# The stores of turned tiles leave the queue of the loads

## The chip, the cores and the metric

The kernel runs on one core of one Trainium2 chip. The metric is device time in microseconds (us) for one execution of the whole program, as a median of several runs. The profile is of one further execution, and its times count from the start of its span. A transfer between the chip's memory (HBM) and the core's own memory is issued by an engine, and carried by 16 DMA engines that serve all queues of the core.

## The reference

A stack of four graph layers works on features x of 5120 nodes by 64 and one matrix adj of 5120 by 5120, all float32. Each layer normalises its input and adds its result to x:

```
h = relu(layernorm(x));  x = x + L0(h, adj)     # e = h + par*(diag*h) @ W
                                                # layernorm(adj @ (adj.T @ e)) * gamma + beta + h
h = relu(layernorm(x));  x = x + adj @ h        # L1
h = relu(layernorm(x));  x = x + L2(h, adj)     # Chebyshev: three products adj @ T, with weights
h = relu(layernorm(x));  x = x + L3(h, adj)     # relu(D^-1/2 (adj + I) D^-1/2 (h @ W + b))
```

L0 needs adj.T @ e, then adj times that; L1, L2 and L3 need five more products by adj.

## The kernel before

adj (105 MB) is handled as 10 x 10 tiles of 512 x 512 float32, 1 MB each. A product by adj contracts over adj's columns, so TensorE must have its tiles turned. The program has two stages.

**The first stage** goes once over adj, by ten groups g of 512 columns and in each by ten tiles m of 512 rows. A raw tile arrives by a load (L327; L313 for the first ten) in `raw[:, m]`. 128 partitions times four rows of 512 floats make 512 pieces of 2 KB. With it TensorE does two things: `products_for_t` (L375) sums adj.T @ e of the column group, and `turn_half` (L412) turns the tile in two halves into PSUM. ScalarE copies each half to `whole[m % 5]` (L570, `copy_turned`). From there the turned tile is used by `multiply` (L366), and it is stored to `adj_t` in HBM (L320, `store`), 8 KB from each partition. VectorE sums the tile's rows (L667, for the degrees) and adds the products up (L699).

In step m of group g TensorE's order is: turn tile m+1 of this group, multiply with turned tile m, then `products_for_t` with raw tile m of the next group. That raw tile overwrites the one turned a step before. Its load is issued as soon as both halves of that one are turned (`half_turned`). So from the load's issue to the need for its data lie one multiply, one product, one turn and another multiply.

**The second stage** makes the five further products in a planned order of tiles. It reads turned tiles back from `adj_t` (303 loads of 1 MB, L332) into 15 buffers. Ten of its loads are issued within the last group of the first stage; the others wait at L351 until every store has landed.

The sync engine (SP) issues all 1 MB transfers, by `group` for groups 0 to 8 (g = 1 to 8 is a loop on the device): `load_next(g, m)` waits for `half_turned`, then `store(g, m)` waits for `half_copied`. Everything that SP issues is in one DMA queue (q1). ScalarE issues eight small loads of weights at the start and, at the end, ten stores of 128 KB of the output (L637); these are in a queue of its own (q10). A buffer `whole[m % 5]` is overwritten five tiles later, once its store has landed (`stored`) and its product is done (`used`).

Of the kernel before, what the change touches and what calls it, by code (L numbers as in the profile page):

```python
# [16 lines left out]
NB = N // B  # L17
# [4 lines left out]
STAGED = 5  # L22
# [129 lines left out]
def gnn_stack(nc, x_d, adj_d, wu_d, du_d, pu_d, wi_d, di_d, pi_d, gam_d, bet_d, w2_d, b2_d, w3_d, b3_d, out_d):  # L152
    plan = Plan()
    ctx = ExitStack()
    with ctx:
        def sb(name, shape, dt=F32, stack=ctx):
            return stack.enter_context(nc.sbuf_tensor(name, shape, dt))

        def sem(name):
            return ctx.enter_context(nc.semaphore(name))  # L160
# [5 lines left out]
        whole = [sb(f"whole{s}", [P, SUB, B]) for s in range(STAGED)]  # L166
# [48 lines left out]
        stored = [sem(f"stored{s}") for s in range(STAGED)]  # L215
# [6 lines left out]
        half_copied = sem("half_copied")  # L222
# [38 lines left out]
        adj_t_v = adj_t.rearrange("m k p a n -> p m k (a n)")  # L261
# [14 lines left out]
        def slot(n):  # L276

            return (STAGED + n) % SLOTS
# [25 lines left out]
        @block.sync  # L304
        def _(sp):
            sp.dma_start(X[:, :, :], x_v).then_inc(x_in, 16)
            for dst, src in ((diag[:, 0:U // P], du_d.rearrange("(t p) -> p t", p=P)),
                             (diag[:, U // P:NT], di_d.rearrange("(t p) -> p t", p=P)),
                             (par[:, 0:2], pu_d.partition_broadcast(P)), (par[:, 2:4], pi_d.partition_broadcast(P)),
                             (w_in[:, 0, :], wu_d), (w_in[:, 1, :], wi_d)):  # L310
                sp.dma_start(dst, src, allow_slow_non_contiguous=True).then_inc(early_in, 16)  # L311
            for m in range(NB):
                sp.dma_start(raw[:, m], adj_v[:, m, :, 0, :]).then_inc(raw_in[m], 16)  # L313

            def store(g, m):
                sp.wait_ge(half_copied, g * (NB * 2) + (2 * m + 2))
                src = whole[m % STAGED][:, :, :].rearrange("p a n -> p (a n)")
                dst = adj_t_v[:, m, g] if isinstance(g, int) else \
                    adj_t_v[:, m, bass.ds(g, 1), :].rearrange("p g n -> p (g n)")
                sp.dma_start(dst, src).then_inc(stored[m % STAGED], 16)  # L320

            def load_next(g, m):

                sp.wait_ge(half_turned, g * (NB * 2) + (2 * m + 2))
                src = adj_v[:, m, :, g + 1, :] if isinstance(g, int) else \
                    adj_v[:, m, :, bass.ds(g + 1, 1), :].rearrange("p a g k -> p a (g k)")
                sp.dma_start(raw[:, m], src).then_inc(raw_in[m], 16)  # L327

            def load_turned(n):

                p, m, k, dual = plan.tiles[n]
                sp.dma_start(whole[slot(n)][:, :, :].rearrange("p a n -> p (a n)"), adj_t_v[:, m, k]) \  # L332
                    .then_inc(whole_in[slot(n)], 16)

            def group(g):
                for m in range(NB):
                    load_next(g, m)
                    store(g, m)

            group(0)  # L340
            with sp.Fori(1, NB - 1) as g:
                group(g)
            for j in range(NB):
                store(NB - 1, j)
                sp.wait_ge(half_turned, (NB - 1) * (NB * 2) + (2 * j + 2))
                sp.wait_ge(deg_summed, (NB - 1) * NB + j + 1)
                p, m, k, dual = plan.tiles[j]
                sp.wait_ge(stored[m % STAGED], 16 * (2 * k + m // STAGED + 1))
                load_turned(j)
            for s in range(STAGED):  # L350
                sp.wait_ge(stored[s], 16 * TOTAL_TILES // STAGED)  # L351
            for n in range(NB, len(plan.tiles)):
                if n < SLOTS:
                    sp.wait_ge(used, TOTAL_TILES - SLOTS + n + 1)
                else:
                    sp.wait_ge(multiplied, plan.used_no(n - SLOTS))
                load_turned(n)
# [179 lines left out]
        def _(act):  # L537
# [26 lines left out]
            def copy_turned(g, m):  # L564
                for h in range(HALVES):
                    act.wait_ge(half_turned, g * (NB * 2) + (2 * m + h + 1))
                    if h == 0 and not (isinstance(g, int) and g * NB + m < STAGED):
                        act.wait_ge(stored[m % STAGED], g * (16 * NB // STAGED) + 16 * (m // STAGED))
                        act.wait_ge(used, g * NB + (m - STAGED + 1))
                    nc.scalar.activation(whole[m % STAGED][:, h * HS:(h + 1) * HS, :], turned[h][:, :, :],  # L570
                                         ACT.Copy).then_inc(half_copied, 1)

            def copy_t(g):
                act.wait_ge(t_done, g + 1)
                if not isinstance(g, int) or g > 0:
                    act.wait_ge(t_turned, g)
                nc.scalar.activation(t_t[:, :], aux[0][:, :], ACT.Copy).then_inc(t_copied, 1)

            def take_t(g):
                act.wait_ge(t_turned, g + 1)  # L580
                if not isinstance(g, int) or g > 0:
                    act.wait_ge(used, g * NB)
                nc.scalar.activation(t_cur[:, :, :], aux_rows[1], ACT.Copy).then_inc(t_ready, 1)

            def end_of_layer(i):

                if i < NB:
                    act.wait_ge(h_rows, i + 1)
                    nc.scalar.activation(E[:, of(i), :], aux_rows[i % 2], ACT.Copy)
                    if i >= 2:  # L590
                        act.wait_ge(var_ready, LN_NO["h", i - 2] + 1)
                    square(("h", i), aux_rows[i % 2], sq[i % 2][:, :, :])
                if 0 <= i - 3 < NB:
                    m = i - 3
                    if m >= 2:
                        act.wait_ge(var_ready, LN_NO["x", m - 2] + 1)
                    square(("x", m), E[:, of(m), :], cen[m % 2][:, :, :])

            def group(g, followed=True):
                take_t(g)  # L600
                for m in range(1, NB + 1):
                    if m < NB or followed:
                        copy_turned(g, m)
                    if not followed and m >= 2:
                        end_of_layer(m - 2)
                if followed:
                    copy_t(g + 1)

            copy_t(0)
            copy_turned(0, 0)  # L610
            group(0)
            with act.Fori(1, NB - 1) as g:
                group(g)
            group(NB - 1, followed=False)


            for s in range(N_STEPS):
                if NB - 1 + s < END_STAGES:
                    end_of_layer(NB - 1 + s)
                for i in plan.part_saved_in.get(s, []):  # L620
                    p, m = plan.dual_rows[i]
# [11 lines left out]
                for r in plan.rows_at(s, 4, 4):  # L633
                    p, m = plan.rows[r]
# [248 lines left out]
```

## Time and profile before

| what | value |
|---|---|
| device time, median of 3 runs | 1684.7 us (1683.16 to 1686.06) |
| device time of the profiled execution | 1682.59 us |
| its span | 1680.8 us |
| TensorE busy, share of the span | 93% |
| ScalarE busy, share of the span | 16% |
| first stage, last raw tile landed at | 639 us |
| DMA traffic | 531 MB |

The span is what the profile shows of the execution; it is 1.8 us shorter than the device time of that execution. "Busy" of TensorE counts a matmul as busy while it is in its pipeline. A time "to landing" is that from a transfer's issue until its last byte has arrived. A share of the DMA is the mean busy share of the 16 engines, and an engine that waits within a packet counts as busy; over short stretches the share comes out slightly over 1.

### The profile page before, as it was taken

Reading aid. Unit: us, or ns where it says so; the run is one execution under the profiler, and the core shown is the slowest. Engines: PE = TensorE matmul, PEld = TensorE weight load, DVE = VectorE, ACT = ScalarE, POOL = GpSimd, SP = SyncE. Lnnn points to the kernel's source line nnn. Section 1 sums busy time; section 2 is a strip of 40 time slices with the busy share of each in tenths; the row PEclk is TensorE's granted clock in tenths of the full one; section 3 lists DMA queues with packets and bytes.
Section 4 is the critical chain, followed back from the end, with each engine's and each line's share of the span. In section 5 each row is a group of like instructions: output and inputs, shape, how many; then the busy total and the mean of one; then the engine's idle time right before and its main releaser. Section 6 shows DMA issues by size and latency. Waiting matters only on the chain.

```text
span 1680.8 us, 19919 instructions
## 1 busy us (share of the span) xinstructions
PE 1570.1 (93%) x8120; PEld 661.5 (39%) x8120; DVE 459.0 (27%) x623; ACT 266.1 (16%) x351; POOL 95.0 (6%) x103
## 2 busy tenths in 40 slices
PE   5889889989988999899999989999999999999798
PEld 3444444434444445433333333333333343333333
DVE  6544444444444444511011010000100031111211
ACT  2233323323232334200000000000000001000000
POOL 2300000000000002800000000000000000000000
PEclk9999999999999999999999999999999999999899
DMA  8599999999999999999888678888676747737997
GB/s 282 176 332 329 321 320 330 326 327 337 323 323 325 333 331 370 409 426 425 335 360 346 251 300 311 290 299 301 256 294 276 310 190 313 294 126 306 424 408 310
DMA packets 124219, 531.27 MB, mean 316 GB/s; under 512 B 20096, under 2 KB 21376, under 8 KB 72576
## 3 DMA queue, kind: packets, MB, share of 16 engines
q1 hardware_dynamic: 117728, 528.83, 84.0%
q10 hardware_dynamic: 6432, 1.57, 0.4%
q8 instruction: 47, 0.77, 0.2%
q14 instruction: 12, 0.10, 0.0%
HBM read 424.20 MB, written 106.17 MB: 316 GB/s over the span
## 4 chain that ended last, share of the span: by engine, by line
PE 71%; DMA 24%; DVE 3%; POOL 1%; issue 1%; SPq 1%; ACT 0%; DVEq 0%; ACTq 0%
PE turned L366 32%; DMA raw<-in_adj_dram 22%; PE acc L366 20%; PE turned L412 6%; PE aux L375 6%; PE aux L501 2%; PE turned L521 1%; DMA out_dram<-sq 1%; PE aux L503 1%; DVE deg_part L667 1%; PE aux L511 1%; SPq L311 1%; PE aux L420 0%; PE aux L431 0%; POOL rstd L827 0%
## 5 line engine op out<-in xcount | busy, mean ns | idle before, releaser
L366 PE MATMUL turned<-whole,F 128*64 128x512 f32 x1184 | 274.3, 595 | 0.0
L375 PE MATMUL aux<-raw,E 128*64 128x512 f32 x800 | 194.8, 608 | 59.9 <-DMA raw<-in_adj_dram 59.7
L570 ACT ACTIVATE whole<-turned 128x1024 f32<-128x1024 f32 x200 | 193.8, 1022 | 356.6 <-PE turned L412 356.6
L366 PE MATMUL turned<-whole,E 128*64 128x512 f32 x1064 | 249.2, 595 | 0.0
L667 DVE TENSOR_REDUCE deg_part<-raw 128x2048 f32 (+1 forms) x100 | 227.7, 2277 | 0.0
L412 PEld LDWEIGHTS turned<-ident,raw 128*128 128x128 f32 x1600 | 173.8, 141 | 75.2 <-issue 73.6
L412 PE MATMUL turned<-ident,raw 128*128 128x128 f32 x1600 | 198.0, 276 | 0.3 <-ACT whole L570 0.3
L366 PE MATMUL acc<-whole,t_cur 128*64 128x512 f32 x800 | 193.7, 605 | 0.0
L699 DVE TENSOR_TENSOR h_acc<-acc,h_acc 128x512 f32<-128x512 f32 x90 | 62.2, 691 | 305.2 <-PE acc L366 305.2
L366 PEld LDWEIGHTS turned<-whole,F 128*64 128x64 f32 x1184 | 82.1, 137 | 154.6 <-issue 151.9
L827 POOL TENSOR_TENSOR rstd<-rstd,minus_half 128x4 f32<-128x4 f32 x50 | 51.7, 1035 | 1447.1 <-DVE rstd L656 1447.0
L366 PE MATMUL acc<-whole,E 128*64 128x512 f32 x536 | 128.1, 601 | 5.6 <-issue 4.7
L366 PE MATMUL acc<-whole,R 128*64 128x512 f32 x560 | 127.5, 593 | 5.1 <-DVE R L660 5.1
L366 PEld LDWEIGHTS turned<-whole,E 128*64 128x64 f32 x1064 | 73.7, 137 | 138.5 <-issue 136.7
L375 PEld LDWEIGHTS aux<-raw,E 128*64 128x64 f32 x800 | 49.3, 137 | 195.6 <-DMA raw<-in_adj_dram 135.3
L624 ACT ACTIVATE part<-turned 128x512 f32<-128x512 f32 x40 | 23.9, 597 | 552.3 <-PE turned L366 534.2
L366 PE MATMUL acc<-whole,F 128*64 128x512 f32 x416 | 98.5, 608 | 0.0
L799 DVE TENSOR_TENSOR y_sb<-acc,part 128x512 f32<-128x512 f32 x24 | 16.5, 689 | 249.1 <-PE acc L366 245.6
L366 PEld LDWEIGHTS acc<-whole,t_cur 128*64 128x64 f32 x800 | 48.5, 136 | 73.8 <-issue 73.7
L366 PEld LDWEIGHTS acc<-whole,R 128*64 128x64 f32 x560 | 40.3, 137 | 82.7 <-issue 82.3
L366 PEld LDWEIGHTS acc<-whole,E 128*64 128x64 f32 x536 | 38.2, 138 | 78.1 <-issue 77.5
L366 PE MATMUL turned<-whole,R 128*64 128x512 f32 x240 | 55.0, 593 | 0.0
(89 smaller groups left out, 560.8 us busy)
## 6 DMA issues: line engine op xcount, KB each, us to landing
whole<-adj_t SPq DMA_DIRECT2D x303, 1024.0 KB, 10.1
raw<-in_adj_dram SPq DMA_DIRECT2D x100, 1024.0 KB, 8.8
adj_t<-whole SPq DMA_DIRECT2D x100, 1024.0 KB, 10.0
out_dram<-sq ACTq DMA_DIRECT2D x10, 128.0 KB, 14.4
fold_weigh<-in_L_gnn_weights_dram ACTq DMA_DIRECT2D x2, 48.0 KB, 2.3
gam<-in_L_gnn_ln_gamma_dram ACTq DMA_DIRECT2D x1, 32.0 KB, 2.8
bet<-in_L_gnn_ln_beta_dram ACTq DMA_DIRECT2D x1, 32.0 KB, 2.9
b<-in_L_gnn_bias_dram ACTq DMA_DIRECT2D x1, 32.0 KB, 4.0
```

What stands on the lines that cost most here:

```text
L311: sp.dma_start(dst, src, allow_slow_non_contiguous=True).then_inc(early_in, 16)
L366: last = nc.tensor.matmul(bank[half, :], v[:, i, :], tile[:, i, :], start=start and i < 2, stop=stop and i >= SUB - 2)
L375: last = nc.tensor.matmul(aux[0][half, :], E[:, m * SUB + a, :], raw[:, m, a, :], start=(m == 0 and a < 2), stop=(m == NB - 1 and a >= SUB ...
L412: last = nc.tensor.transpose(turned[h][:, b, a * P:(a + 1) * P], raw[:, m % NB, a, (h * HS + b) * P:(h * HS + b + 1) * P], ident[:, :])
L501: last = nc.tensor.matmul(y_wide[:, a, :], turned_y, fold_weigh[:, p - 1, :], start=True, stop=True)
L503: last = nc.tensor.matmul(aux_rows[0][:, a, :], turned_y, fold[:, :], start=True, stop=True)
L511: last = nc.tensor.transpose(aux[1][0:D, a * P:(a + 1) * P], SOURCE[p][:, m * SUB + a, :], ident[:, :])
L570: nc.scalar.activation(whole[m % STAGED][:, h * HS:(h + 1) * HS, :], turned[h][:, :, :], ACT.Copy).then_inc(half_copied, 1)
L624: nc.scalar.activation(part[:, m, :], dual_bank[i % 2], ACT.Copy).then_inc(part_saved, 1)
L667: nc.vector.tensor_reduce(out, raw[:, m], AX.X, ALU.add).then_inc(deg_summed, 1)
L699: ins = nc.vector.tensor_tensor(h_acc[:, m, :], acc[m % 2][:, :], h_acc[:, m, :], ALU.add)
L827: op.tensor_tensor(v, v, minus_half[:, 0:SUB], ALU.pow).then_inc(pow_ready, 1)
```

## The change

`store` moves from the sync engine's program to ScalarE's. It waits for the same count of `half_copied` and issues the same transfer with the same semaphore, in ScalarE's queue. ScalarE calls it right behind the two copies of a tile. SP keeps the loads, with their waits. No transfer changes in size or address, and nothing changes on TensorE, VectorE and GpSimd.

```
             def group(g):
                 for m in range(NB):
                     load_next(g, m)
-                    store(g, m)
...
             for j in range(NB):
-                store(NB - 1, j)
                 sp.wait_ge(half_turned, (NB - 1) * (NB * 2) + (2 * j + 2))
...
+            def store(g, m):
+                act.wait_ge(half_copied, g * (NB * 2) + (2 * m + 2))
+                src = whole[m % STAGED][:, :, :].rearrange("p a n -> p (a n)")
+                dst = adj_t_v[:, m, g] if isinstance(g, int) else \
+                    adj_t_v[:, m, bass.ds(g, 1), :].rearrange("p g n -> p (g n)")
+                act.dma_start(dst, src).then_inc(stored[m % STAGED], 16)
...
                     if m < NB or followed:
                         copy_turned(g, m)
+                        store(g + m // NB, m % NB)
                     if not followed and m >= 2:
                         end_of_layer(m - 2)
...
             copy_t(0)
             copy_turned(0, 0)
+            store(0, 0)
             group(0)
```

SP's instructions in group 0, which is written out, stand like this before (`raw<-in_adj_dram` is a raw load, `adj_t<-whole` a store; the five rows here are issued over two and a half tiles, and in brackets is what each waits for):

```order
L327 DMA raw<-in_adj_dram 128x4x512 [waits half_turned]
L320 DMA adj_t<-whole0 128x2048 [waits half_copied]
L327 DMA raw<-in_adj_dram 128x4x512 [waits half_turned]
L320 DMA adj_t<-whole1 128x2048 [waits half_copied]
L327 DMA raw<-in_adj_dram 128x4x512 [waits half_turned]
```

In the changed kernel, whose line for the raw load is L320, the first ten raw loads are followed by group 0's ten, and then by the device's loop:

```order
L313 DMA raw<-in_adj_dram 128x4x512 x10
L320 DMA raw<-in_adj_dram 128x4x512 [waits half_turned] x10
L333 UNCONDITIONAL_BRANCH
L333 ISA
L320 ISA [waits half_turned]
L320 DMA raw<-in_adj_dram 128x4x512
```

No store is left among SP's loads. On ScalarE the end of the same group stands like this before (`whole<-turned` is the copy of one half of a tile):

```order
L570 ACTIVATE whole3<-turned0 128x1024 [waits used,stored3,half_turned]
L570 ACTIVATE whole3<-turned1 128x1024 [waits half_turned]
L570 ACTIVATE whole4<-turned0 128x1024 [waits used,stored4,half_turned]
```

And in the changed kernel, whose line for the copy is L561 and for the store L569:

```order
L569 DMA adj_t<-whole3 128x2048 [waits half_copied]
L561 ACTIVATE whole4<-turned0 128x1024 [waits used,stored4,half_turned]
L561 ACTIVATE whole4<-turned1 128x1024 [waits half_turned]
L569 DMA adj_t<-whole4 128x2048 [waits half_copied]
L561 ACTIVATE whole0<-turned0 128x1024 [waits used,stored0,half_turned]
```

The store has come between the second half of a tile and the wait for the first half of the next.

## Rows read from the trace of the kernel before

**Rows 1.** The page: busy time by engine, and the chain that ended last.
```profile
span 1680.8 us, 19919 instructions
PE 1570.1 (93%) x8120; PEld 661.5 (39%) x8120; DVE 459.0 (27%) x623; ACT 266.1 (16%) x351; POOL 95.0 (6%) x103
...
PE 71%; DMA 24%; DVE 3%; POOL 1%; issue 1%; SPq 1%; ACT 0%; DVEq 0%; ACTq 0%
PE turned L366 32%; DMA raw<-in_adj_dram 22%; PE acc L366 20%; PE turned L412 6%; PE aux L375 6%; PE aux L501 2%; PE turned L521 1%; DMA out_dram<-sq 1%; PE aux L503 1%; DVE deg_part L667 1%; PE aux L511 1%; SPq L311 1%; PE aux L420 0%; PE aux L431 0%; POOL rstd L827 0%
```

**Rows 2.** Stretches: length, busy time by engine, TensorE's clock, DMA share, GB/s.
```profile
22.00:38.00 16.00, 15.06 (x75) 7.97 (x76) 15.69 (x26) 3.61 (x7) 3.33 (x3) 1.00 1.05 408
64.00:640.00 576.00, 516.12 (x2938) 249.25 (x2938) 258.39 (x180) 181.70 (x197) 10.69 (x6) 1.00 0.97 328
640.00:700.00 60.00, 56.21 (x358) 33.32 (x354) 30.59 (x73) 27.65 (x49) 37.32 (x47) 1.00 0.97 389
700.00:750.00 50.00, 48.61 (x236) 18.55 (x238) 10.55 (x28) 3.39 (x7) 13.94 (x12) 1.00 1.01 426
```

**Rows 3.** The chain of waits, 297 to 316 us: start, length, what.
```profile
297.70 8.97 DMA raw<-in_adj_dram
306.67 0.04 issue
306.71 1.94 PE aux L375 x8
308.65 1.91 PE turned L412 x16
...
310.71 8.77 DMA raw<-in_adj_dram
```

**Rows 4.** Who waited for whom, 64 to 640 us: total us, times, longest.
```profile
ACT whole L570 <- PE turned L412: 354.0, 81, 5.6
PE aux L375 <- DMA raw<-in_adj_dram: 59.7, 75, 2.1
```

**Rows 5.** The raw loads, line L327: issues, then time to landing.
```profile
L327 SPq DMA_DIRECT2D raw<-in_adj_dram x90: 367/378/393, 62.1 to 630.1; - x90
...
DMA to landing us min/median/max: 6.9/8.7/9.4
```

**Rows 6.** The stores, line L320: issues, then time to landing.
```profile
L320 SPq DMA_DIRECT2D adj_t<-whole x100: 332/363/924, 63.2 to 681.2; - x100
...
DMA to landing us min/median/max: 4.9/10.0/11.1
```

**Rows 7.** What SP issued at 310 to 319 us: start, length, line.
```profile
310.71 0.38 SPq L327 DMA_DIRECT2D raw<-in_adj_dram  x1
311.88 0.36 SPq L320 DMA_DIRECT2D adj_t<-whole  x1
316.84 0.38 SPq L327 DMA_DIRECT2D raw<-in_adj_dram  x1
318.07 0.37 SPq L320 DMA_DIRECT2D adj_t<-whole  x1
```

**Rows 8.** DMA queues, 1582 to 1592 us: packets, MB, share of 16 engines.
```profile
q1 hardware_dynamic: 560, 4.06, 96.2%
q10 hardware_dynamic: 560, 0.14, 6.2%
```

**Rows 9.** The output's stores, line L637, issued by ScalarE: issues, then landing.
```profile
L637 ACTq DMA_DIRECT2D out_dram<-sq x10: 378/378/417, 1575.7 to 1678.4; - x10
...
DMA to landing us min/median/max: 1.9/14.4/20.3
```

**Rows 10.** ScalarE, 310.5 to 317.5 us: start, length, line, idle before.
```profile
309.79 1.94 ACT L570 ACTIVATE whole<-turned 128x1024 f32<-128x1024 f32 x2 [4.67 <-PE turned L412]
315.97 1.94 ACT L570 ACTIVATE whole<-turned 128x1024 f32<-128x1024 f32 x2 [4.24 <-PE turned L412]
```

**Rows 11.** ScalarE's small loads of weights, one of eight: issue length in ns.
```profile
L562 ACTq DMA_DIRECT2D fold_weigh<-in_L_gnn_weights_dram x2: 633/646/658, 54.0 to 54.7; - x2
```

More of the change, by code:

```diff
@@ L313, in _ @@
                 sp.dma_start(raw[:, m], adj_v[:, m, :, 0, :]).then_inc(raw_in[m], 16)
[L315 to L320, printed above, removed]
             def load_next(g, m):
@@ L337, in group @@
                     load_next(g, m)
-                    store(g, m)
             group(0)
@@ L343, in _ @@
             for j in range(NB):
-                store(NB - 1, j)
                 sp.wait_ge(half_turned, (NB - 1) * (NB * 2) + (2 * j + 2))
@@ L571, in copy_turned, with store @@
                                          ACT.Copy).then_inc(half_copied, 1)
+            def store(g, m):
+                act.wait_ge(half_copied, g * (NB * 2) + (2 * m + 2))
+                src = whole[m % STAGED][:, :, :].rearrange("p a n -> p (a n)")
+                dst = adj_t_v[:, m, g] if isinstance(g, int) else \
+                    adj_t_v[:, m, bass.ds(g, 1), :].rearrange("p g n -> p (g n)")
+                act.dma_start(dst, src).then_inc(stored[m % STAGED], 16)
             def copy_t(g):
@@ L603, in group @@
                         copy_turned(g, m)
+                        store(g + m // NB, m % NB)
                     if not followed and m >= 2:
@@ L610, in _ @@
             copy_turned(0, 0)
+            store(0, 0)
             group(0)
```

## The prediction

> **What bounds the kernel now.** I read the engines' busy time and the chain first. TensorE is busy for 93% of the span, yet 22% of the chain is transfers of raw tiles [rows 1], and those exist only in the first stage. Next the stretches: from 64 to 640 us the DMA share is 0.97 at 328 GB/s, while raw loads alone ran at 408 GB/s (22 to 38 us) and loads of turned tiles alone at 426 GB/s (700 to 750 us) [rows 2]. So the first stage holds the DMA engines almost all the time, at a lower rate than either kind of load reaches alone. The chain there repeats one loop: a raw load (8.77 to 8.97 us), its product (1.94), the turn that follows (1.91), and at once the next load [rows 3]. That loop spans two tiles. With about 0.1 of issue, 2T = L + 3.95, where T is the time per tile and L a raw load's time to landing. With the median L of 8.7 [rows 5] T is 6.33; the 90 loads were issued from 62.1 to 630.1 us [rows 5], so T was 568.0/89 = 6.38. What could be gained here at most is what TensorE's products wait for raw tiles, 59.7 us [rows 4].
>
> **The issue moves to ScalarE.** 100 issues of 0.36 us leave SP [rows 6]. SP's raw loads don't come sooner for it: the store was issued 1.2 us after its load and the next load only 5 us later [rows 7], so SP stood waiting for the turn. On ScalarE an issue costs 0.38 us [rows 9] to 0.65 us [rows 11], with a wait for its own copy. Behind the store stands the wait for the next tile's first half, and before that ScalarE is idle for 4.2 to 4.7 us [rows 10]; in all it waited 354 us there in 81 waits [rows 4]. Cost 0. Without that cover it would be 100 x 0.65 = 65 us. In the last group SP issues its turned loads without standing behind the store's wait for the copy, by about 1 us at most; TensorE doesn't wait for these loads, since it waited for no transfer but raw tiles. Gain 0.
>
> **The queues.** This is the term that decides. Before, one queue holds load, store, load, store in order. Per tile a store was issued 1.2 us behind its load [rows 7] and landed in 10.0 us [rows 6], so 11.2 after that load's issue and 11.2 - 6.4 = 4.8 after the next load's. The load before landed 8.7 - 6.4 = 2.3 after it. So on the DMA engines that end last, each raw load stood first behind the rest of the load before it, then behind the whole store before it (4.8 - 2.3 = 2.5 us, against 1.05 MB / 426 GB/s = 2.46), and then ran. The store of its own tile came behind it.
>
> With two queues both have work. How the DMA engines share themselves then is shown at the end of the program, where ScalarE's output stores run beside SP's loads: in 10 us 560 packets of one queue and 560 of the other, though one kind has 8 KB and the other 256 bytes [rows 8]. They take one packet of each in turn, whatever its size. A 128 KB output store, which lands in 1.9 us at the quickest, took 14.4 at the median and 20.3 at most [rows 9]. Per DMA engine, a raw load is 32 packets of 2 KB and a store 8 packets of 8 KB. Turn by turn the store is through after 8 of the load's 32 packets: it overtakes. The load's own store, 2.46 us of service, now comes in the load's way and no longer behind it. The store before it is out of the way earlier, but it took that time from the load before, whose rest stands there instead. The work ahead at a load's issue is thus the same, and L grows by 2.46 us at the same T.
>
> Then T grows, and gives the queues time to drain. Let k us of the work ahead go for each us by which T is longer: 2d = 2.46 - k d, or d = 2.46 / (2 + k). With k = 0 (the work ahead stays) d = 1.23; k = 1 gives 0.82, k = 2 gives 0.62, k = 4 gives 0.41. If the same DMA engine were the last each time, the relief would pile up until nothing is ahead, and d would be 0. I take k = 2: a load spans 8.7/6.4 = 1.4 tiles and a store 10.0/6.4 = 1.6, so that up to two tiles' relief arrives within one load. 90 tiles have a raw load beside a store: 90 x 0.62 = **+55 us**, bounds 90 x 0.41 = +37 and 90 x 1.23 = +111.
>
> **The mix of reads and writes.** At the rates of loads alone a tile would need 1.05/0.408 + 1.05/0.426 = 5.0 us; it takes 6.4, so 1.4 us per tile go to something that comes with reads and writes together. Before, each DMA engine has a run of 32 reads and then a run of 8 writes; now it alternates for part of the time. No row shows what that does to the 1.4 us. If all of it went, TensorE's waits would go, -60 us; if it grew by half, T would be up to 0.7 longer, +63. I take 0, since 16 DMA engines out of step mix the two at the memory already.
>
> **Later stages.** The ten loads of turned tiles in the last group have 8 KB packets like the stores, so the two share evenly. Everything after 700 us is unchanged. TensorE's clock was at 1.00 in all stretches up to 750 us, where it was busy for 90% of the first stage [rows 2]; with T at 7.0 it would be 83%, and I count nothing for that.
>
> **Sum.** 1682.6 + 55 = 1738 for the profiled execution; its time lies 2.1 us below the median of the runs. So 1740, for the likeliest case from 1715 to 1795.
>
> **Rivals.**
> 1. *Order doesn't matter, capacity does.* The DMA share is 0.97 [rows 2] and no byte changes. If the last DMA engine is simply full, k is large and T stays at 6.4: 1685, within 4 us. For it: the share. Against it: the loop also closes by L alone, with L nearly constant at 8.7 to 9.4, and anything that lengthens L is paid at half. The Trainium skill, "DMA: Bandwidth & Descriptors", under Rules for kernel authors, says that spreading transfers over several issuing engines brings no bandwidth, as they share the same 16 DMA engines and interleave, and saves only issue time. By that rule, taken alone, the time stays at 1685; the alternation of packets in the rows agrees with the interleaving it describes. Chance 0.12.
> 2. *Faster.* The 1.4 us per tile are in part time in which a DMA engine waits for a read to come back. With a second queue it could move a store's packets meanwhile. Each us off the tile's service first pays the 2.46 us back, then takes TensorE's waits. It decides from where more than about 1.2 us of the 1.4 go; then the time is between 1625 (all 60 us of waits gone) and 1680, say 1660. For it: loads alone lose almost nothing (408 GB/s), so the loss is of the mix. Against it: the reads' data still comes through the same engines. Chance 0.14.
> 3. *Slower still.* Alternating on one DMA engine raises the loss of the mix by more than 0.5 us, on top of the overtaking: 1800 or more. Chance 0.08.
> 4. *The change doesn't do what it says*, because ScalarE's stores fall into the order of the old queue anyway. [Rows 8] show separate queues being served in turn; chance under 0.02, counted with rival 1, with the same 1685.
>
> **How the numbers follow.** About 0.2% (3.4 us) is what a measurement of this kernel can tell from no change. The likeliest case has 0.66, and rival 3, also slower, 0.08: slower 0.74. Rival 1 gives same 0.12, rival 2 faster 0.14. The range reaches down to 1680, so that it holds rival 1, and up to 1795, the bound with k = 0. It leaves out most of rival 2 and rival 3.
>
> **What would show it.** Right: in the first stage the raw loads land in about 10 us (8.7 before), the stores in about 7 (10.0 before); the loop of the chain stays, at about 14 us per two tiles; the last raw load is issued near 685 us (630 before); the DMA share falls below 0.95 at some 300 GB/s; the wait of the products for raw tiles grows to some 115 us; and the last 980 us stay as they are. Wrong by rival 1: loads land later and stores sooner, but T stays 6.4. Wrong by rival 2: the GB/s from 64 us on rise above 328 and the waits of L375 shrink. If ScalarE's idle time before a copy vanishes, or TensorE waits for `half_copied`, then the issue was not free and this working is wrong at its first step.

## The result, and the profile after

The changed kernel takes 1744.9 us at the median of four runs (1736.2 to 1753.35); the kernel before takes 1684.5. The ratio is 1.0365, with a 95% interval from 1.0339 to 1.0391: slower by 60 us, where 55 were forecast. The profiled execution has a span of 1742.3 us, 61.5 more than before.

The first rows are those of the raw loads (L320 in the changed kernel) and of the stores (L569), answering to [rows 5] and [rows 6].

```profile
L320 SPq DMA_DIRECT2D raw<-in_adj_dram x90: 367/373/393, 62.2 to 685.6; - x90
...
DMA to landing us min/median/max: 5.7/9.8/11.3
```

```profile
L569 ACTq DMA_DIRECT2D adj_t<-whole x100: 338/343/362, 63.3 to 738.3; - x100
...
DMA to landing us min/median/max: 7.0/8.8/12.7
```

A raw load lands 1.1 us later at the median (9.8, before 8.7), a store 1.2 us sooner (8.8, before 10.0). The last raw load is issued at 685.6 us, before at 630.1. So the loop over 90 tiles takes 55.5 us longer, 7.00 us per tile for 6.38. From the issue of the last raw load to the end of the span it is 1056.7 us, before 1050.7. Those 6 us are no effect that can be told: in the other runs with the whole second stage this rest is between 1050 and 1059 us, whatever their loop takes.

The next row is the stretch of the loop, with the columns of [rows 2]. The two after it are waits in the same stretch, answering to [rows 4]: TensorE's for raw tiles, and ScalarE's ahead of its copies.

```profile
64.00:680.00 616.00, 525.87 (x2862) 258.41 (x2863) 251.04 (x174) 177.15 (x192) 10.41 (x6) 0.94 0.87 298
```

```profile
PE aux L366 <- DMA raw<-in_adj_dram: 93.1, 49, 4.0
ACT whole L561 <- PE turned L403: 411.8, 81, 10.4
```

The DMA engines are busy for 0.87 of the time and no longer 0.97, at 298 GB/s for 328. Divided by the share, a busy engine works as fast as before (298/0.87 = 343, 328/0.97 = 338 GB/s). What they lost is not speed but work to do: 0.13 of their time they now stand idle. TensorE's waits for raw tiles are fewer (49 for 75) and longer (up to 4.0 us for 2.1), 33 us more in all. ScalarE's idle time before its copies has grown by 58 us; the issue of the stores has cost it nothing.

The clock is the other thing in that row: 0.94 for 1.00. This is the product that follows a long wait, and the turn behind it (TensorE's timeline near 230 us: start, length, line, idle before).

```profile
229.05 3.00 PE L366 MATMUL aux<-raw,E 128*64 128x512 f32 x8 [3.22 <-DMA raw<-in_adj_dram]
231.98 2.54 PE L403 MATMUL turned<-ident,raw 128*128 128x128 f32 x16
234.45 1.94 PE L357 MATMUL acc<-whole,t_cur 128*64 128x512 f32 x8
```

Behind 3.22 us without a matmul, the product took 3.00 us for 1.94 and the turn 2.54 for 1.97. In this stretch of 8 us the clock stood at 0.79 on average, a mix of its two levels (2.4 and 1.2 GHz), and then at 1.00 again:

```profile
228.00:236.00 8.00, 6.95 (x32) 3.51 (x34) 0.77 (x1) 1.94 (x2) 0.00 (x0) 0.79 0.66 241
236.00:247.00 11.00, 11.00 (x66) 5.43 (x62) 5.77 (x4) 3.88 (x4) 0.00 (x0) 1.00 0.94 304
```

Over the program this shows in the products with raw tiles and in the turns. Of the kernel before, then after:

```profile
L412 PE MATMUL turned<-ident,raw 128*128 128x128 f32 x1600 | 198.0, 276 | 0.3 <-ACT whole L570 0.3
L375 PE MATMUL aux<-raw,E 128*64 128x512 f32 x800 | 194.8, 608 | 59.9 <-DMA raw<-in_adj_dram 59.7
```

```profile
L366 PE MATMUL aux<-raw,E 128*64 128x512 f32 x800 | 215.1, 663 | 93.2 <-DMA raw<-in_adj_dram 93.1
...
L403 PE MATMUL turned<-ident,raw 128*128 128x128 f32 x1600 | 207.4, 284 | 0.3 <-ACT whole L561 0.3
```

They are busy for (215.1 - 194.8) + (207.4 - 198.0) = 30 us more. With the 33 us of waits that makes 63 us, where the span grew by 61.5: an account of TensorE's time, and not yet of causes. Whether those 30 us are a cause, or lie in time that the loop would have waited anyway, the filler runs below take up.

The packets of the two queues can be seen side by side. Take the load issued at 245.65 us and its store, issued at 246.81 (each row ends with the time to landing in us):

```profile
raw<-in_adj_dram SPq DMA_DIRECT2D x1, 1024.0 KB, 10.9
```

```profile
adj_t<-whole ACTq DMA_DIRECT2D x1, 1024.0 KB, 8.6
```

The store lands at 255.4, the load only at 256.5. From 252 to 253 us these two are the only transfers in progress (the queues' packets, MB and share):

```profile
q10 hardware_dynamic: 41, 0.34, 79.2%
q1 hardware_dynamic: 39, 0.08, 20.5%
```

41 packets of the store and 39 of the load: nearly equal numbers, and 0.34 MB of the store for 0.08 MB of the load. This is [rows 8] again, now with a store against a load.

It doesn't happen to every tile. The store issued at 235.78, 1.1 us behind its load, has no packet in progress before 239, though its queue is empty. From 236 to 239 us the load has the engines to itself. It moves 389 of its 512 packets and lands in 5.9 us:

```profile
q1 hardware_dynamic: 389, 0.80, 90.2%
```

Counting the packets of each kind in order over the 90 tiles, a store's first packet starts 3.6 us after its issue at the median, and by then 386 of the 512 packets of its own load have started. A store lands ahead of its own load in 33 tiles of 90; in the kernel before in none. So the overtaking is real, but partial, and it hits some tiles and spares others.

Where the chain goes through a raw load it keeps its form, here with loads of 10.9 and 10.7 us (8.97 and 8.77 in [rows 3]) and 14.9 us for two tiles:

```profile
245.65 10.87 DMA raw<-in_adj_dram
256.51 0.04 issue
256.55 1.94 PE aux L366 x8
258.49 1.91 PE turned L403 x16
...
260.55 10.69 DMA raw<-in_adj_dram
```

But it goes through fewer of them. Between the issues of the first and the last of the 90 loads the chain held 42 raw loads of 8.7 us on average, so nearly every second tile. Now it holds 31, of 10.2 us. Over all 90 the mean time to landing is 9.1 us (8.7 before), though the median is 9.8: many loads are slow, and some are quick, at about 6 us. The quick ones give little back, because a tile takes TensorE 5.5 us in any case.

### The profile page after: what moved, and what is told of

The parts are those of the page before. It is cut to its first block, busy times and chain, and to the rows that moved or that the text cites. A ratio compares the mean times of both kernels' runs of the same rounds, so it can differ in the third digit from the quotient of the medians.

```text
span 1742.3 us, 19927 instructions
## 1 busy us (share of the span) xinstructions
PE 1601.0 (92%) x8120; PEld 678.3 (39%) x8120; DVE 459.1 (26%) x623; ACT 266.6 (15%) x351; POOL 95.1 (5%) x103
## 4 chain that ended last, share of the span: by engine, by line
PE 75%; DMA 20%; DVE 2%; POOL 1%; issue 1%; SPq 1%; ACT 0%; DVEq 0%; ACTq 0%
PE turned L357 31%; PE acc L357 22%; DMA raw<-in_adj_dram 19%; PE aux L366 8%; PE turned L403 8%; PE aux L492 2%; PE turned L512 1%; DMA out_dram<-sq 1%; PE aux L494 1%; PE aux L502 1%; SPq L311 1%; DVE deg_part L667 1%; PE aux L422 0%; PE turned L389 0%; POOL rstd L827 0%
## 5 line engine op out<-in xcount | busy, mean ns | idle before, releaser
L366 PE MATMUL aux<-raw,E 128*64 128x512 f32 x800 | 215.1, 663 | 93.2 <-DMA raw<-in_adj_dram 93.1
L561 ACT ACTIVATE whole<-turned 128x1024 f32<-128x1024 f32 x200 | 194.2, 1021 | 414.6 <-PE turned L403 414.4
L403 PEld LDWEIGHTS turned<-ident,raw 128*128 128x128 f32 x1600 | 183.2, 146 | 86.3 <-issue 85.5
L403 PE MATMUL turned<-ident,raw 128*128 128x128 f32 x1600 | 207.4, 284 | 0.3 <-ACT whole L561 0.3
L366 PEld LDWEIGHTS aux<-raw,E 128*64 128x64 f32 x800 | 55.4, 146 | 226.5 <-DMA raw<-in_adj_dram 141.6
```

Source lines behind the costliest of these rows:

```text
L366: last = nc.tensor.matmul(aux[0][half, :], E[:, m * SUB + a, :], raw[:, m, a, :], start=(m == 0 and a < 2), stop=(m == NB - 1 and a >= SUB ...
L403: last = nc.tensor.transpose(turned[h][:, b, a * P:(a + 1) * P], raw[:, m % NB, a, (h * HS + b) * P:(h * HS + b + 1) * P], ident[:, :])
```

## The experiments

**The theory**: in a queue of its own, a store gets one packet per turn like the load, but its packets are four times as large. It takes the engines' time from the load whose data TensorE waits for, and can get through ahead of it. **Rivals**: alternating between reads and writes costs in itself; the second queue has a fixed price; the lower clock is the cost.

### The size of the packets

Three kernels cut the store in smaller pieces; what is stored, and where, stays the same. A store becomes two transfers, one of every other piece; the counts waited for on `stored` double.

```
+                src = src.rearrange("p (a b n) -> p a b n", b=2, n=512)
...
-                act.dma_start(dst, src).then_inc(stored[m % STAGED], 16)
+                dst = dst.rearrange("p (a b n) -> p a b n", b=2, n=512)
+                for b in range(2):
+                    act.dma_start(dst[:, :, b], src[:, :, b]).then_inc(stored[m % STAGED], 16)
```

n=512 makes 2 KB pieces, n=256 makes 1 KB pieces. The control does the same with 2 KB in the kernel before (`sp` for `act`).

> The kernel before, its one queue kept, with each store cut in packets of 2 KB: two transfers of half a MB, each of every other 2 KB piece. Control for the next two. Overtaking theory (what costs is that in a queue of its own a store gets through ahead of the raw load, since the DMA engines take packets in turn): nothing can overtake here, so only the smaller packet costs, 0.1 us of service and 0.4 us of issue per tile that SP has idle: 1685 to 1697. Rival theory (what costs is the alternation of reads and writes by itself, packet by packet): the same here.

> The changed kernel with each store cut in packets of 2 KB, as in the control. Overtaking theory: a store now gets 32 packets of a DMA engine's turns against the load's 32, not 8; it starts 1.2 us behind the load and no longer gets through ahead of it, so the load loses about 1.6 us and not 2.46: raw loads land in about 9.3 us (9.8 in the changed kernel), time 1710 to 1730. Rival (alternation costs): four times as many switches between reads and writes, so not below the changed kernel's 1745, rather 1750 to 1780.

> The same with packets of 1 KB: the load moves 2 KB for each 1 KB of the store, so the load has the advantage. Overtaking theory: the load loses at most some 1.2 us; raw loads land under 9 us, stores in 11 or more; time 1690 to 1715, the lowest of the three with two queues. Rival: eight times the switches, 1760 or more.

Measured against the kernel before (1685.5 us beside these runs): one queue, 2 KB: 1661.5 us, ratio 0.9872 (0.9849 to 0.9895). Two queues, 2 KB: 1678.0, 0.9955 (0.9939 to 0.9971). Two queues, 1 KB: 1663.4, 0.9867 (0.9839 to 0.9896).

The control missed: it is 24 us faster than the kernel before, where a small loss was expected by both theories. Both runs with two queues are below the whole range expected for them, too. So the comparison has to be made pair by pair. With the same packets, the second queue costs 60 us at 8 KB and 17 at 2 KB. The one-queue partner at 1 KB was run later:

> The kernel before, one queue, stores in packets of 1 KB (two transfers each). One-queue partner of the run with 1 KB in two queues (1663). If what is left of the second queue's cost goes with the packet's size (60 us at 8 KB, 17 at 2 KB), it is under 10 us here: 1653 to 1668. If it is a fixed price of the second queue, some 17 us: 1640 to 1650.

It takes 1657.0 us, 0.9833 (0.9801 to 0.9865); the second queue costs 6 us at 1 KB, less than the two intervals can tell from nothing. 60, 17, 6: the cost goes with the size of the store's packets. The more pieces, the more often reads and writes can alternate, and yet the cost falls from left to right. Neither the alternation nor a fixed price of the queue can be the main cost. In the two kernels with two queues and small packets no store lands ahead of its own load, where with 8 KB 33 of 90 did. The rows of L320 in the two-queue kernels, at 2 KB and at 1 KB, show the landing:

```profile
L320 SPq DMA_DIRECT2D raw<-in_adj_dram x90: 367/373/393, 62.7 to 622.3; - x90
...
DMA to landing us min/median/max: 5.8/8.6/9.7
```

```profile
L320 SPq DMA_DIRECT2D raw<-in_adj_dram x90: 367/373/392, 63.0 to 607.6; - x90
...
DMA to landing us min/median/max: 5.8/8.2/9.1
```

With 8 KB it was 9.8 at the median and 11.3 at most. The stores with 1 KB were expected in 11 us or more, and landed in 9.8.

Why smaller packets help in one queue was then the question. Control: two transfers per store, but of 64 partitions each, with 8 KB packets.

```
-                sp.dma_start(dst, src).then_inc(stored[m % STAGED], 16)
+                for b in range(2):
+                    sp.dma_start(dst[b * 64:(b + 1) * 64], src[b * 64:(b + 1) * 64]).then_inc(stored[m % STAGED], 16)
```

> The kernel before, one queue, each store as two transfers of 64 partitions, 8 KB packets. Control for the gain of 24 us with 2 KB packets in one queue. If that gain comes from the size of the packets, this is 1680 to 1690. If it comes from having two transfers per store, 1655 to 1670.

1677.6 us, 0.9968 (0.9954 to 0.9981), between the two ranges expected: some 7 of the 24 us come with two transfers of this kind, the rest only with smaller packets. What does it inside a DMA engine stays open. The row of the stretch from 64 to 640 us of the one-queue kernel with 2 KB shows the engines with a share of 1.00 at 346 GB/s, so the gain is time in which they had stood idle (0.97 before) as well as a little speed:

```profile
64.00:640.00 576.00, 541.99 (x3130) 268.88 (x3130) 268.96 (x198) 197.07 (x220) 19.96 (x18) 1.00 1.00 346
```

### Half of the change

```
                     load_next(g, m)
-                    store(g, m)
+                    if m % 2:
+                        store(sp, g, m)
...
                         copy_turned(g, m)
+                        if m % 2 == 0:
+                            store(act, g + m // NB, m % NB)
```

> Half of the change: stores of even tiles are issued by ScalarE in its queue, those of odd tiles by SP in the old one, 8 KB packets. Both theories: about half of the loss, 1705 to 1725. If the loss is mostly TensorE's lower clock after long waits, which sets in only past some length of a wait, less than half: under 1705.

1743.0 us, 1.0352 (1.0335 to 1.0369): half of the stores moved, and the whole loss. Neither expectation holds. The trace offers a reading in which the theory stands. The loop goes from a raw load over its product and the turn behind it to the raw load two tiles on. A group has ten tiles, so even tiles form one loop and odd tiles another, tied together by TensorE's order. By this reading the slower loop sets the pace of both, and here every even load has its own store in the other queue. The chain shows it: between 100 and 690 us it holds 31 raw loads, and each of them is one that ScalarE's store follows within 2 us, that is, an even one. Three of them, and ScalarE's stores in the same stretch:

```profile
315.69 11.01 DMA raw<-in_adj_dram
...
330.74 8.26 DMA raw<-in_adj_dram
...
343.06 10.97 DMA raw<-in_adj_dram
```

```profile
316.83 0.34 ACTq L309 DMA_DIRECT2D adj_t<-whole  x1
331.91 0.34 ACTq L309 DMA_DIRECT2D adj_t<-whole  x1
344.29 0.34 ACTq L309 DMA_DIRECT2D adj_t<-whole  x1
```

No odd load is in the chain. SP's own stores, of the odd tiles, stand between them (326.15, 337.39 us). Even loads take 9.2 us on average, odd ones 8.7. A run with the odd stores moved instead, which could put this to the test, was not made.

### When the store is issued

The changed kernel with one more wait ahead of the store, on TensorE's product and VectorE's sum of the tile before. Nothing is released by it. It puts the issue 1.4 us later: 2.6 us behind the load, where it was 1.2.

```
                 act.wait_ge(half_copied, g * (NB * 2) + (2 * m + 2))
+                act.wait_ge(h_added, g * NB + m)
```

> The changed kernel, 8 KB packets and two queues, but each store also waits until the product of the tile before is added up, so that it is issued some 3 us behind its raw load and not 1.1. Overtaking theory: the load is mostly through by then and the store is done before the next load's first packets, so raw loads land in under 9 us again and the time falls to 1680 to 1715. If the second queue costs in itself (more loss in the mix of reads and writes, or the issue on ScalarE), where the store stands in time changes little: 1740 to 1750.

1670.7 us, 0.9911 (0.9879 to 0.9942). That is below the whole range expected, 74 us less than the changed kernel, with the same two queues, the same packets and the same engine, and less than the kernel before. Below are its raw loads and its stretch from 64 to 640 us.

```profile
L320 SPq DMA_DIRECT2D raw<-in_adj_dram x90: 367/373/393, 62.3 to 618.7; - x90
...
DMA to landing us min/median/max: 5.0/7.9/11.5
```

```profile
64.00:640.00 576.00, 523.91 (x3006) 261.10 (x3005) 263.28 (x183) 186.45 (x203) 11.10 (x6) 0.99 0.91 335
```

Loads land in 7.9 us at the median. A fixed price of the second queue, or of the issue on ScalarE, can't be what cost the 60 us: both are still there.

How the later issue helps is clear only in part. A store now finds 420 of its load's 512 packets started when its own first packet starts (386 in the changed kernel, both at the median). In the worst tenth of the tiles it is 366 or fewer, where it was 219 or fewer. So the load is further ahead, as the theory has it. But the store is not done before the next load begins, as the expectation had it: it lands 3.3 us after that load's issue at the median, and 3.2 in the changed kernel. And two things changed that the theory doesn't speak of. The store's first packet starts 1.6 us after its issue and no longer 3.6 (3.7 in the kernel before, with one queue). And a busy DMA engine moves more: 335/0.91 = 368 GB/s, against 338 before and 343 in the changed kernel. That is not because loads and stores overlap less: both kinds have packets in progress for 3.9 us per tile in either kernel. The share of these two in the 74 us is open.

The same wait with smaller packets asks whether the two cures add up.

> Both changes that helped, together: two queues, the store issued some 3 us behind its load, packets of 2 KB. If they cure different things (overtaking, and reads held up beside 8 KB packets) they add up: 1645 to 1660, and period per tile under 6.1 us. If both only work by lifting the store out of the load's way, no better than the better of them: 1661 to 1671.

> The same with packets of 1 KB. Adding up: 1645 to 1660. Not adding up: 1661 to 1671.

With 2 KB: 1653.8 us, 0.9821 (0.979 to 0.9852). With 1 KB: 1654.9, 0.9852 (0.9799 to 0.9905). Both lie in the range expected if the two cures add up. The first is the lowest time of the study, 30 us below the kernel before. The one-queue kernel with 1 KB (ratio 0.9833) is within its interval, so for a kernel as simple as possible the second queue isn't needed.

### The stores taken away, nearly

```
-                src = whole[m % STAGED][:, :, :].rearrange("p a n -> p (a n)")
+                src = whole[m % STAGED][:, :, :].rearrange("p a n -> p (a n)")[:, 0:256]
...
-                sp.dma_start(dst, src).then_inc(stored[m % STAGED], 16)
+                sp.dma_start(dst[:, 0:256], src).then_inc(stored[m % STAGED], 16)
```

> The kernel before with stores of an eighth (1 KB from each partition, 128 KB per tile); the second stage then reads tiles of adj itself, in 2 KB pieces. It leaves out that the products of the second stage use turned tiles. It shows the loop of raw loads without stores in the way: if the loop is held up by the service of stores, raw loads land in 5 to 6 us, TensorE waits for none, and the last raw load is issued at about 575 us (630 before); the second stage, with slower loads, is not compared.

```profile
L327 SPq DMA_DIRECT2D raw<-in_adj_dram x90: 367/378/393, 62.7 to 556.6; - x90
...
DMA to landing us min/median/max: 5.0/5.2/6.4
```

Loads land in 5.2 us, and the last is issued at 556.6 us, 5.55 us per tile. It was expected at about 575. That is the loop with TensorE as its limit; its products' waits for raw tiles are down to 1.4 us in all. By this single run the stores cost the kernel before 630.1 - 556.6 = 74 us of the first stage.

### The clock

Four transposes whose result isn't used go on TensorE ahead of its wait for the raw tile, in the changed kernel and in the kernel before.

```
+                        for _i in range(4):
+                            nc.tensor.transpose(aux[1][:, 2 * P:3 * P], ident[:, :], ident[:, :])
                         products_for_t(g + 1, m)
```

> The changed kernel with four more transposes (0.48 us) on TensorE in each tile of the first stage, ahead of the wait for the raw tile; their result is not used. If the lower clock behind long waits adds its 30 us to the time, and the waits can hold the filler, then the clock comes back to 0.98 or more and the time is 1715 to 1735 in spite of 43 us more work. If the clock's share is hidden in the loop anyway, or the filler doesn't hold the clock, 1745 to 1765.

> The kernel before, one queue, with the same filler of four transposes (0.48 us per tile) on TensorE. Its clock is at 1.00 in the first stage as it is, so this gives the filler's own price. If the filler is free beside waits (they are 0.66 us per tile on average), 1684 to 1690: then the clock that came back in the changed kernel with filler, at an unchanged time, was worth nothing. If the filler costs 10 to 30 us here, the clock's return may have paid for that there, and the clock's share in the loss is of that size.

In the changed kernel: 1743.2 us, 1.036 (1.0338 to 1.0383), the same as without filler and in neither range expected. The clock of its loop is back to 0.99, and its products and turns take (215.1 - 202.1) + (207.4 - 200.8) = 20 us less:

```profile
64.00:680.00 616.00, 561.25 (x3213) 282.92 (x3214) 251.06 (x174) 177.46 (x193) 11.21 (x6) 0.99 0.89 300
```

```profile
L366 PE MATMUL aux<-raw,E 128*64 128x512 f32 x800 | 202.1, 628 | 54.8 <-DMA raw<-in_adj_dram 54.3
...
L403 PE MATMUL turned<-ident,raw 128*128 128x128 f32 x1600 | 200.8, 279 | 0.3 <-ACT whole L563 0.3
```

In the kernel before, the filler makes it 1692.7 for 1686.5 us, 1.004 (1.0022 to 1.0058): some 7 us, between the two cases expected. So 43 us of filler are nearly free there, because they stand in time that was waits (59.7 us before, 10.2 with filler). If it costs the same in the changed kernel, where the time didn't change at all, then the clock's return paid for those 7 us; by the intervals it may be 1 to 14. The rest of the 30 us of slower matmuls lay where the loop waited for its load. That the filler costs the same in both was not measured.

## Why the prediction was right

**The issue on ScalarE** was costed at nothing and cost nothing: an issue takes 0.34 us, and ScalarE's idle time before its copies grew.

**The loop of two tiles**, 2T = L + 3.95, carried the sum. (The pieces between load and load in [rows 3] add up to 4.04 rather than 3.95, which makes no odds.) With the median L of 9.8 it gives T = 6.9; 7.0 was forecast and 7.00 measured. But this is closer than the step deserves. With the mean L of 9.1 it gives 6.5, and in the chain the loop closes through 31 loads and no longer through 42. What was not thought of is the spread of L. The loop doesn't run at an even 14 us per two tiles, but in bursts: a few tiles at TensorE's pace, 5.5 us each, and then one or two that wait, mostly 1.7 to 3.9 us (nine waits between 200 and 330 us). Quick loads don't pay back what slow ones cost.

**The overtaking** was the right mechanism. That packets of two queues get turns in equal numbers was read off the output's stores at the end of the program, and the loop shows the same where a load and a store meet. Packet size (60, 17, 6 us) tells it from alternation and from a fixed price; the later issue (74 us back) tells it from a fixed price again. The term is +55.5 us in the issue of the last raw load, where +55 stood. That closeness is luck in two ways: k = 2 was a choice between bounds of +37 and +111, and it stood for an even loop that isn't there.

**The clock** was left out ("I count nothing for that"), with the mean busy share still 83% (85% was measured). What counted was the single wait: behind 3.22 us without a matmul the clock was at its lower level for a while. The step failed in its reading of the rows, though by the filler runs its price is some 7 us. With it goes a size: the waits were to grow to 115 us and grew to 93, beside 30 us of slower matmuls that had not been counted.

**The stores** were to land in about 7 us and took 8.8. The steps had a store slip through its own load after 8 of the load's 32 packets per DMA engine. It starts too late for that: 3.6 us after its issue, with 386 of 512 packets (24 of 32) of the load under way. So it lands ahead of its own load in 33 tiles and not in all.

**The mix of reads and writes** was taken as unchanged, and was: 338 and 343 GB/s per busy engine. The choice between its bounds was right for this change. But the term is no constant of the kernel: with the later issue it was 368 GB/s.

**Rival 1** (capacity alone) falls with the DMA share of 0.87, and with it the reading of the Trainium skill's rule by which it stood ("DMA: Bandwidth & Descriptors", Rules for kernel authors). That spreading transfers over issuing engines brings no bandwidth agrees with the trace (343 GB/s per busy engine time for 338). That it therefore only saves issue time doesn't: here it changed how the transfers share the engines, at a price of 60 us. **Rivals 2 and 3** fall with the nearly unchanged speed of a busy engine and with the time, 1744.9 us.

## What to carry to other kernels

When two kinds of transfer share the DMA engines, ask which of them someone waits for, and which has the larger packets. In separate queues, where both had packets ready, they got turns in equal numbers (560 and 560, 41 and 39), and so the share of bytes went by packet size: keep the packets of the others no larger than those of the urgent ones, or issue the others when the urgent ones are further on. Both were measured here only with this kernel's tiles of 1 MB. And in a loop that is closed by a transfer's time to land, moving the same bytes in another order can cost or give more than any issue time saved.

## What the runs showed that was not expected

- Stores with 2 KB packets in one queue are faster than with 8 KB, although each byte takes as long or longer alone (loads of 2 KB pieces ran at 408 GB/s, of 8 KB at 426): 1661.5 us for 1685.5. Two transfers per store, by halves of the partitions, gave 7 us; the rest is open.
- Half of the stores in the second queue cost as much as all of them (1743.0 and 1744.9 us), and the chain then runs through even tiles alone: one slow loop of two seems to be enough.
- A wait added ahead of the stores, for nothing that they need, took 74 us off. A store issued 2.6 us behind a load had its first packet 1.6 us later, one issued 1.2 us behind it only after 3.6 us. Why is open.
